# Two of every four message tiles gathered by TensorE, with one-hot comparisons four chunks wide

## The chip, the cores and the metric

The kernel runs on one core of one Trainium2 chip. The metric is the device time of one execution in microseconds (us). The kernel before was run three times: 3272.55, 3278.92 and 3280.07 us, median 3278.92. One further execution was profiled, and its trace is what the rows below are read from.

## The reference

A graph of 3,125 nodes with 64 features and 103,125 edges, sorted by destination, goes through four residual layers. The change lies in the last one, and in a piece of preparation placed inside the third. The last layer computes, with `h = relu(layernorm(x))`:

```python
edge_in = concatenate([edge_feat, hid[src]], axis=1)
msg = relu(edge_in @ W1 + b1)
msg_sum = segment_sum(msg, dst, num_segments=3125)
reduced = msg_sum / maximum(count, 1)
x = x + relu(concatenate([reduced, hid], axis=1) @ W2 + b2)
```

The term `hid[src] @ W1[64:] + b1` is worked out once per node by the stage before, as a table with one row per node (`message_table` in device memory, `gt` in SBUF). So an edge needs the row of its source node, plus its own feature product, then the relu and the sum by destination.

## The kernel before

Edges are taken in tiles of 256 (`TE`), two halves of 128. There are 403 tiles (`T1`). Sums by destination go over blocks of 64 nodes; each visit of a block by a tile is one step of sums, 451 in all (`V2`). `stage_messages` is one loop written out for every engine; at step i TensorE does, in this order:

- the product of edge features of tile t = i (L2088; L2082 on a "picked" tile),
- the pick matmuls that `chunks_of_step(i)` lists (L2095),
- the sums of visit v = i - 2, four instructions (L2104).

A tile gets its source rows in one of two ways. On an ordinary tile GpSimd gathers them from device memory with two indirect DMAs (L2056), up to 8 tiles ahead, and VectorE adds them to the product (L2186). On a picked tile TensorE makes them: `on_pe(t)` says which, the last two of every `GP` = 7 tiles from the second seven on. For the two picked tiles of a group (512 edges) VectorE compares the 512 source indices, less a shift, with the node numbers of each of 25 chunks of 128 nodes (L2192, one instruction a chunk, giving a 128 x 512 one-hot matrix in float16). TensorE multiplies each one-hot with that chunk of the table, split into two float16 halves (L2095), adding the 25 into one bank. ScalarE copies the sum to `hT` (L2122), and TensorE adds it onto the tile's product through `comb` (L2085).

SP loads the 512 indices, broadcast to all partitions, as int32 (L2046); ScalarE turns them into float16 keys with the partition's own number taken off (L2117). 32 one-hot buffers go round. Two banks hold products (`psM`), four hold sums (`psA`), two hold picked rows (`psH`). ScalarE also makes the one-hots of the destinations (L2137, L2143) and applies the relu (L2131, L2128); VectorE adds each visit's sums to the accumulator (L2198). `split()` on VectorE (L2161 to L2174) makes the two float16 halves of the table once, at its step 3; TensorE's first pick waits for it.

Three stages earlier, `stage_attend_tables` prepares the attention layer. Its engines work side by side and the stage ends when the last of them is done; GpSimd's three additions (L1407 to L1411) stand at its end.

Of the kernel before, what the change touches and what calls it, by code (L numbers as in the profile page):

```python
# [8 lines left out]
F16 = mybir.dt.float16  # L9
# [8 lines left out]
P = 128  # L18
NODES = 3125
EDGES = 103125  # L20
D = 64
# [1286 lines left out]
CENTER = NODES // 2  # L1308
AG = 16
# [45 lines left out]
def stage_attend_tables(nc, m, keep, s_in, x_out, q_out, w_in, w1, w2, w3, bp, bb2, b3, g2, b2, b1, x_t, q_t):  # L1355

    with ExitStack() as ctx:
# [11 lines left out]
        s_wt = sem("at_wt"); s_u = sem("at_u"); s_wo = sem("at_wo"); s_zero = sem("at_zero")  # L1369
        turned = sem("at_turned"); copied = sem("at_copied"); q_done = sem("at_q_done"); q_ready = sem("at_q")  # L1370
# [6 lines left out]
        def _(sp):  # L1377
# [10 lines left out]
            for g in range(NG):  # L1388
                sp.wait_ge(x_taken0, g + 1)
                sp.wait_ge(x_taken1, g + 1)  # L1390
                j = slice(2 * GROUP * g, 2 * GROUP * g + 2 * len(chunks(g)))
                sp.dma_start(q_t[j, :, :].rearrange("j p n -> p j n"), q_all[:, j, :]).then_inc(q_out, 16)
            sp.wait_ge(w_in, WEIGHTS_IN)
# [54 lines left out]
        def _(act):  # L1448
            act.wait_ge(s_zero, 2)
# [20 lines left out]
        def _(dve):  # L1470
# [8 lines left out]
            ins.then_inc(s_wo, 1)  # L1479
            dve.tensor_reduce(gm, hn.rearrange("p a d -> p (a d)"), op=ALU.max, axis=X, apply_absolute_value=True).then_inc(m.max_in, 1)  # L1480
            dve.wait_ge(s_zero, 2)
            for g in range(NG + 1):
                if g < NG:
# [3 lines left out]
                    dve.tensor_scalar(qf[g % 2][:, 0:n], m.PB[2 + g % 2][:, 0:n], bq_c, float(D) ** -0.5, ALU.add, ALU.mult).then_inc(q_ready, 1)  # L1487
                if g >= 1:
# [475 lines left out]
GP = 7  # L1964
HOT = 32
# [17 lines left out]
def chunks_of_step(i):  # L1983

    return [(q, a) for q, t in enumerate(chains()) for u in range(GP) if i == t - 5 + u for a in range(u * NCH // GP, (u + 1) * NCH // GP)]


def stage_messages(nc, m, keep, w1, w_out, b_out, o_in, ef_t, src, g_t):

    with ExitStack() as ctx:  # L1990
# [16 lines left out]
        hot = [take(TE).bitcast(F16) for _ in range(HOT)]  # L2007
        keyI = [take(2 * TE).bitcast(I32) for _ in range(2)]
        key = [take(TE).bitcast(F16) for _ in range(2)]
        hT = [take(TE).bitcast(F16) for _ in range(2)]  # L2010
        down, downI = take(1), m.colsN[:, 7, 0:1].bitcast(I32)
        gmax, gtop, one_row = take(1), take(1, 1), take(P, 1)
        wexp = take(1).bitcast(I32)
        psM = [halves(m.PB[0][:, 0:2 * D]), halves(m.PB[1][:, 0:2 * D])]
        psA = [m.PB[2 + i][0:BD, 0:MW] for i in range(4)]
# [9 lines left out]
        key_ready, hot_ready, hot_used, h_copied = m.key_ready, m.hot_ready, m.hot_used, m.h_copied  # L2025
# [5 lines left out]
        def _(sp):  # L2031
# [3 lines left out]
            for t in range(T1):  # L2035
# [6 lines left out]
                if t % GP == 0 and on_pe(t + 2 * GP - 2):  # L2042
                    q = chains().index(t + GP)
                    wait(sp, key_ready, Q0 + q - 1)
                    edges = src[(t + 2 * GP - 2) * TE:(t + 2 * GP) * TE]
                    sp.dma_start(keyI[q % 2], edges.partition_broadcast(P)).then_inc(m.landed_q[q % 2], 16)  # L2046
# [14 lines left out]
        def _(pe):  # L2061
# [7 lines left out]
            for i in range(V2 + 2):  # L2069
                t = i  # L2070
                if t < T1:
                    pe.wait_ge(m.landed_e[t % R], before(t) + landed(t))
                    if t >= 2:
                        if on_pe(t - 2):
                            pe.wait_ge(m_ready, t - 1)
                        else:
                            pe.wait_ge(added, pool_tiles(t - 1))
                    both = psM[t % 2].rearrange("p s c -> p (s c)")
                    if on_pe(t):
# [3 lines left out]
                        for s in range(2):  # L2083
                            e = (t % GP - (GP - 2)) * TE + s * P
                            ins = pe.matmul(psM[t % 2][:, s, :], hT[q % 2][:, e:e + P], comb, start=False, stop=True, skip_group_check=True)  # L2085
# [3 lines left out]
                for q, a in chunks_of_step(i):  # L2089
# [5 lines left out]
                    pe.matmul(psH[q % 2], table[:, a, :, :].rearrange("p s d -> p (s d)"), hot[n % HOT],  # L2095
                              start=(a == 0), stop=(a == NCH - 1)).then_inc(hot_used, 1)
                v = i - 2
                if v >= 0:
# [3 lines left out]
                    wait(pe, acc_ready, v - 3)  # L2102
                    for s in range(2):
                        ins = pe.matmul(psA[v % 4], oh[v % 4][:, s, :], M[:, bass.ds(slot, 1), s, :].rearrange("p t c -> p (t c)"),  # L2104
# [257 lines left out]
```

## Time and profile before

| | |
|---|---|
| median of three runs | 3278.92 us |
| profiled execution: its own time | 3277.56 us |
| profiled execution: span of the instructions | 3275.8 us |
| message tiles, first to last product (L2088) | 2422.85 to 3196.26 us |
| message stage's sums after the last tile, then output | 3201.79 to 3275.8 us |
| busy share of the span, TensorE / VectorE / ScalarE / GpSimd | 82 / 67 / 50 / 48 % |

The span leaves out 1.8 us of the execution's own time. Busy shares are means over all four layers; the change acts on about a quarter of the span, and what bounds that quarter must be read from its own stretch. "PE" is TensorE's matmuls, "PEld" its weight loads, "DVE" VectorE, "ACT" ScalarE, "POOL" GpSimd, "SP" the queue that issues most transfers.

### The profile page before, as it was taken

The numbers are of one execution on the slowest core, as the hardware profiler recorded it, in microseconds if no ns is written. First come the engines' busy times: TensorE is split into PE (matmuls) and PEld (weight loads), VectorE is DVE, ScalarE is ACT, GpSimd is POOL, SyncE is SP. The second block draws the span as 40 slices with busy tenths as digits, with TensorE's granted clock in tenths as the row PEclk, the third lists the DMA queues.
The fourth block names the chain that finished last, engine by engine and source line by source line (L and its number), as shares of the span: only waits on it lengthen the run. The fifth ranks groups of instructions, "written<-read, shape, count | busy, mean of one in ns | idle before, by whom it ended". The sixth has DMA issues, their size and how long they took to land. (4 is left out here: it accounts for less than half of the span.)

```text
span 3275.8 us, 70668 instructions
## 1 busy us (share of the span) xinstructions
PE 2693.3 (82%) x18331; PEld 1815.5 (55%) x18331; DVE 2187.2 (67%) x7716; ACT 1623.9 (50%) x4731; POOL 1571.5 (48%) x1644
## 2 busy tenths in 40 slices
PE   2777777799996799488889888899968888888888
PEld 1566665455553344267777777777844444444446
DVE  6999997566665224567777777777876565566552
ACT  1788886133332000145555555555655555555555
POOL 2111110144442000277777777776037777777770
PEclk6999999899998899689999999999879999999995
DMA  1222222255558766233333333333123333333320
GB/s 37 76 89 89 91 89 74 66 196 198 199 197 322 304 241 240 73 75 85 80 81 84 81 80 85 81 80 72 29 54 82 80 79 79 79 79 79 79 69 13
DMA packets 412218, 349.46 MB, mean 107 GB/s; under 512 B 174824, under 2 KB 342984, under 8 KB 411880
## 3 DMA queue, kind: packets, MB, share of 16 engines
q1 hardware_dynamic: 360296, 286.03, 27.6%
q0 software_dynamic: 42176, 44.91, 7.1%
q10 hardware_dynamic: 9408, 14.34, 1.2%
q8 instruction: 173, 2.83, 0.4%
q14 instruction: 165, 1.35, 0.1%
HBM read 259.07 MB, written 86.00 MB: 105 GB/s over the span
## 5 line engine op out<-in xcount | busy, mean ns | idle before, releaser
L1579 POOL DMA_INDIRECT big<-row_table,src x710 | 676.7, 953 | 217.3 <-issue 169.9
L2056 POOL DMA_INDIRECT big<-message_table,src x582 | 605.8, 1041 | 242.2 <-issue 174.1
L507 PE MATMUL banks<-work 128*128 128x226 f16 x1197 | 312.5, 261 | 104.8 <-ACT banks L538 43.7
L2095 PE MATMUL banks<-big 128*128 128x512 f16 x1400 | 372.4, 384 | 7.6 <-DVE big L2174 7.6
L2192 DVE TENSOR_SCALAR big<-big 128x512 f16<-128x512 f16 x1400 | 349.3, 307 | 28.9 <-ACT big L2117 28.3
L899 PE MATMUL banks<-big,work 128*128 128x512 f16 (+1 forms) x1750 | 344.4, 354 | 17.0 <-DVE work L1041 17.0
L964 POOL TENSOR_TENSOR work<-work 128x400 f16<-128x400 f32 x196 | 180.3, 946 | 272.4 <-DVE work L1033 205.8
L1724 DVE TENSOR_REDUCE big<-banks 128x1 f32<-128x256 f32 x451 | 190.3, 422 | 172.7 <-PE banks L1622 159.6
L1622 PE MATMUL banks<-big 97*128 x902 | 302.5, 418 | 0.0
L508 PE MATMUL banks<-work 128*128 128x200 f16 x1197 | 300.8, 251 | 0.0
L509 PE MATMUL banks<-work 128*128 128x200 f16 x1197 | 298.7, 250 | 0.0
L2186 DVE TENSOR_TENSOR big<-banks,big 128x128 f32<-128x128 f32 x291 | 84.0, 289 | 285.3 <-issue 174.8
L1665 ACT ACTIVATE big<-big 128x1 f32<-128x1 f32 x451 | 91.5, 203 | 351.6 <-DVE big L1735 339.4
L2137 ACT ACTIVATE big<-iotaH,rel 128x64 f32<-128x64 f16 x902 | 259.0, 335 | 5.2 <-DVE big L2151 3.6
L450 POOL COPY work<-work 128x100 f16<-128x100 f16 x120 | 70.2, 586 | 398.2 <-DVE work L473 379.1
L2104 PEld LDWEIGHTS banks<-big 128*64 128x64 f32 x1804 | 152.5, 147 | 192.2 <-issue 191.1
L899 PEld LDWEIGHTS banks<-big,work 128*128 128x128 f16 x1750 | 156.0, 100 | 184.4 <-DVE work L1041 17.3
L2131 ACT ACTIVATE big<-big 128x128 f32<-128x128 f32 x291 | 89.9, 309 | 332.5 <-DVE big L2186 315.0
L1115 PE MATMUL banks<-big,work 128*128 128x512 f16 x900 | 203.4, 387 | 56.2 <-DVE work L1199 52.1
L2104 PE MATMUL banks<-big 128*64 x1804 | 216.9, 247 | 22.8 <-issue 11.7
L1605 PE MATMUL banks<-ident,big 128*97 128x128 f32 x710 | 146.7, 290 | 100.1 <-issue 69.5
L928 ACT CAST work<-work 128x400 f16<-128x400 f32 x196 | 100.7, 525 | 240.2 <-DMA work<-weights_dense 239.5
(372 smaller groups left out, 6293.9 us busy)
## 6 DMA issues: line engine op xcount, KB each, us to landing
big<-weights_halves SPq DMA_DIRECT2D x10, 6400.0 KB, 24.0
weights_dense<-work SPq DMA_DIRECT2D x196, 200.0 KB, 1.9
work<-weights_dense SPq DMA_DIRECT2D x196, 200.0 KB, 2.6
weights_halves<-work SPq DMA_DIRECT2D x98, 400.0 KB, 2.7
big<-q_table SPq DMA_DIRECT2D x451, 64.0 KB
big<-in_ef SPq DMA_DIRECT2D x403, 64.0 KB
big<-in_src SPq DMA_DIRECT2D x56, 256.0 KB
big<-in_ea SPq DMA_DIRECT2D x403, 32.0 KB
```

Source lines behind the costliest of these rows:

```text
L507: pe.matmul(to(CW, CW + CAW), rows[:, 0, t, :], cols[:, t, :], start=False, stop=True, skip_group_check=True)
L508: pe.matmul(to(0, CW), rows[:, 1, t, :], cols[:, t, 0:CW], start=False, stop=True, skip_group_check=True)
L509: pe.matmul(to(0, CW), rows[:, 2, t, :], cols[:, t, 0:CW], start=False, stop=True, skip_group_check=True).then_inc(vis_done, 1)
L899: ins = pe.matmul(m.PB[c % 4][:, 0:width(c)], z[k][:, a, :, :], m.counts(c)[:, a, :], start=(a == 0), stop=(a == NCH - 1))
L1115: pe.matmul(out, z[l % 2][:, a, :, :], weights[:, :, s, a * BP:(a + 1) * BP], start=(a == 0 and s == 0), stop=False)
L1579: po.indirect_dma_start(rows[:, t % RT, s, 0:D], None, x_t.rearrange("a p c -> (a p) c"), bass.IndirectOffsetOnAxis(ap=m.src2[:, s, t:t + ...
L1622: pe.matmul(psS[v % 3], qT[v % R][0:XW, :], XF[0:XW, bass.ds(slot, 1), :].rearrange("p t e -> p (t e)"), start=False, stop=True).then_inc( ...
L2056: po.indirect_dma_start(G[n % R][:, s, :], None, g_t.rearrange("a p c -> (a p) c"), bass.IndirectOffsetOnAxis(ap=m.src2[:, s, t:t + 1], ax ...
L2095: pe.matmul(psH[q % 2], table[:, a, :, :].rearrange("p s d -> p (s d)"), hot[n % HOT], start=(a == 0), stop=(a == NCH - 1)).then_inc(hot_u ...
L2104: ins = pe.matmul(psA[v % 4], oh[v % 4][:, s, :], M[:, bass.ds(slot, 1), s, :].rearrange("p t c -> p (t c)"), start=(s == 0), stop=(s == 1))
L2137: ins = nc.scalar.activation(away[v % 2][:, s, :], m.iotaH[:, 0:BD], ACT.Abs, bias=m.rel2[:, s, v:v + 1], scale=-1.0)
L2192: dve.tensor_scalar(hot[n % HOT], key[q % 2], float(P * a - CENTER), None, ALU.is_equal).then_inc(hot_ready, 1)
```

## The change

- `GP` goes from 7 to 4: the last two of every four tiles are picked, and the 25 chunks of a group's chain are spread over four steps instead of seven (6, 6, 6 and 7 of them).
- The comparisons come in batches of four chunks: five shifted float16 copies of all source indices (`src - CENTER - 128 k`, k = 0 to 4) are made once, in `stage_attend_tables`, and written to device memory (`keys_t`). A group's keys are loaded as five rows of 512 per partition; one instruction compares four rows with one number per partition (`place`), which stands for chunks a to a + 3. Six instructions of 2048 columns and one of 512 replace 25 of 512.
- ScalarE's conversion L2117 is gone, with its semaphore; SP's key load waits for the comparisons of the group before last.
- One one-hot buffer per chunk (25) instead of 32 in rotation.
- Three banks for products and three for sums, instead of two and four; the waits on them follow.
- `split()` comes at VectorE's step 2 instead of 3.
- New in `stage_attend_tables`: a load of `src` from ScalarE's queue, five VectorE instructions of 806 columns, a 1 MB write to `keys_t` on SP's queue, and SP's wait until it has landed.

The diff, with signatures and the parts that only pass names through left out:

```diff
@@ -1306,6 +1306,7 @@
 CENTER = NODES // 2
+SHIFTS = 5
 AG = 16
@@ -1367,6 +1368,9 @@
         s_wt = sem("at_wt"); s_u = sem("at_u"); s_wo = sem("at_wo"); s_zero = sem("at_zero")
+        s_keys = sem("at_keys")
+        srcI = take(EPAD // P).bitcast(I32)
+        shifted = take(SHIFTS * EPAD // P // 2).bitcast(F16).rearrange("p (k f) -> p k f", k=SHIFTS)
         turned = sem("at_turned"); copied = sem("at_copied"); q_done = sem("at_q_done"); q_ready = sem("at_q")
@@ -1390,6 +1394,10 @@
                 sp.dma_start(q_t[j, :, :].rearrange("j p n -> p j n"), q_all[:, j, :]).then_inc(q_out, 16)
+                if g == NG - 3:
+                    sp.wait_ge(s_keys, SHIFTS)
+                    sp.dma_start(keys_t.rearrange("k (p f) -> p k f", p=P), shifted).then_inc(m.first_landed[1], 16)
+            sp.wait_ge(m.first_landed[1], 32)
             sp.wait_ge(w_in, WEIGHTS_IN)
@@ -1446,6 +1454,7 @@
         def _(act):
+            act.dma_start(srcI, src.rearrange("(p f) -> p f", p=P)).then_inc(m.first_landed[0], 16)
             act.wait_ge(s_zero, 2)
@@ -1477,6 +1486,8 @@
             ins.then_inc(s_wo, 1)
+            dve.wait_ge(m.first_landed[0], 32)
+            dve.tensor_scalar(shifted[:, 0, :], srcI, float(-CENTER), None, ALU.add).then_inc(s_keys, 1)
             dve.tensor_reduce(gm, hn.rearrange("p a d -> p (a d)"), op=ALU.max, axis=X, apply_absolute_value=True).then_inc(m.max_in, 1)
@@ -1485,6 +1496,10 @@
                     dve.tensor_scalar(qf[g % 2][:, 0:n], m.PB[2 + g % 2][:, 0:n], bq_c, float(D) ** -0.5, ALU.add, ALU.mult).then_inc(q_ready, 1)
+                if 1 <= g < SHIFTS:
+                    if g == 1:
+                        dve.wait_ge(s_keys, 1)
+                    dve.tensor_scalar(shifted[:, g, :], shifted[:, 0, :], float(-P * g), None, ALU.add).then_inc(s_keys, 1)
                 if g >= 1:
@@ -1961,8 +1976,10 @@
-GP = 7
-HOT = 32
+GP = 4
+BATCHES = ((0, 4), (4, 4), (8, 4), (12, 4), (16, 4), (20, 4), (24, 1))
+STEP_BATCHES = (BATCHES[0:2], BATCHES[2:4], BATCHES[4:5], BATCHES[5:7])
+KEY_ROW = 2 * TE + 2
@@ -1982,10 +1999,15 @@
-    return [(q, a) for q, t in enumerate(chains()) for u in range(GP) if i == t - 5 + u for a in range(u * NCH // GP, (u + 1) * NCH // GP)]
-
-
-def stage_messages(nc, m, keep, w1, w_out, b_out, o_in, ef_t, src, g_t):
+    return [(q, a) for q, t in enumerate(chains()) for u in range(GP) if i == t - GP + 1 + u for a in range(u * NCH // GP, (u + 1) * NCH // GP)]
+
+
+def batch_of_step(i):
+
+    return [(q,) + b for q, t in enumerate(chains()) if 0 <= i - t + GP - 1 < GP for b in STEP_BATCHES[i - t + GP - 1]]
+
+
+def stage_messages(nc, m, keep, w1, w_out, b_out, o_in, ef_t, keys_t, g_t):
@@ -2004,15 +2026,15 @@
         comb = take(D // 2).bitcast(F16)
-        hot = [take(TE).bitcast(F16) for _ in range(HOT)]
-        keyI = [take(2 * TE).bitcast(I32) for _ in range(2)]
-        key = [take(TE).bitcast(F16) for _ in range(2)]
+        hot = take(NCH * TE).bitcast(F16)
+        key = [take(SHIFTS * KEY_ROW // 2).bitcast(F16).rearrange("p (k e) -> p k e", k=SHIFTS)[:, :, 0:2 * TE] for _ in range(2)]
+        place = take(len(BATCHES))
         hT = [take(TE).bitcast(F16) for _ in range(2)]
-        down, downI = take(1), m.colsN[:, 7, 0:1].bitcast(I32)
+        downI = m.colsN[:, 7, 0:1].bitcast(I32)
         gmax, gtop, one_row = take(1), take(1, 1), take(P, 1)
         wexp = take(1).bitcast(I32)
-        psM = [halves(m.PB[0][:, 0:2 * D]), halves(m.PB[1][:, 0:2 * D])]
-        psA = [m.PB[2 + i][0:BD, 0:MW] for i in range(4)]
+        psM = [halves(m.PB[i][:, 0:2 * D]) for i in range(3)]
+        psA = [m.PB[3 + i][0:BD, 0:MW] for i in range(3)]
         psH = [m.PB[6], m.PB[7]]
@@ -2022,7 +2044,7 @@
         acc_ready = sem("ms_acc")
-        key_ready, hot_ready, hot_used, h_copied = m.key_ready, m.hot_ready, m.hot_used, m.h_copied
+        hot_ready, hot_used, h_copied = m.hot_ready, m.hot_used, m.h_copied
         Q0, N0 = len(PICKS), NCH * len(PICKS)
@@ -2041,9 +2063,12 @@
                     q = chains().index(t + GP)
-                    wait(sp, key_ready, Q0 + q - 1)
-                    edges = src[(t + 2 * GP - 2) * TE:(t + 2 * GP) * TE]
-                    sp.dma_start(keyI[q % 2], edges.partition_broadcast(P)).then_inc(m.landed_q[q % 2], 16)
+                    if q == 0:
+                        sp.wait_ge(m.first_landed[1], 32)
+                    if q >= 2:
+                        sp.wait_ge(hot_ready, N0 + NCH * (q - 1))
+                    edges = keys_t[:, (t + 2 * GP - 2) * TE:(t + 2 * GP) * TE]
+                    sp.dma_start(key[q % 2], edges.partition_broadcast(P)).then_inc(m.landed_q[q % 2], 16)
@@ -2070,19 +2095,19 @@
                     pe.wait_ge(m.landed_e[t % R], before(t) + landed(t))
-                    if t >= 2:
-                        if on_pe(t - 2):
-                            pe.wait_ge(m_ready, t - 1)
+                    if t >= 3:
+                        if on_pe(t - 3):
+                            pe.wait_ge(m_ready, t - 2)
                         else:
-                            pe.wait_ge(added, pool_tiles(t - 1))
-                    both = psM[t % 2].rearrange("p s c -> p (s c)")
+                            pe.wait_ge(added, pool_tiles(t - 2))
+                    both = psM[t % 3].rearrange("p s c -> p (s c)")
                     if on_pe(t):
...
                             e = (t % GP - (GP - 2)) * TE + s * P
-                            ins = pe.matmul(psM[t % 2][:, s, :], hT[q % 2][:, e:e + P], comb, start=False, stop=True, skip_group_check=True)
+                            ins = pe.matmul(psM[t % 3][:, s, :], hT[q % 2][:, e:e + P], comb, start=False, stop=True, skip_group_check=True)
                         ins.then_inc(m_done, 1)
@@ -2092,16 +2117,16 @@
                     pe.wait_ge(hot_ready, N0 + n + 1)
-                    pe.matmul(psH[q % 2], table[:, a, :, :].rearrange("p s d -> p (s d)"), hot[n % HOT],
+                    pe.matmul(psH[q % 2], table[:, a, :, :].rearrange("p s d -> p (s d)"), hot[:, 2 * TE * a:2 * TE * (a + 1)],
                               start=(a == 0), stop=(a == NCH - 1)).then_inc(hot_used, 1)
...
                     pe.wait_ge(oh_ready, v + 1)
-                    wait(pe, acc_ready, v - 3)
+                    wait(pe, acc_ready, v - 2)
                     for s in range(2):
-                        ins = pe.matmul(psA[v % 4], oh[v % 4][:, s, :], M[:, bass.ds(slot, 1), s, :].rearrange("p t c -> p (t c)"),
+                        ins = pe.matmul(psA[v % 3], oh[v % 4][:, s, :], M[:, bass.ds(slot, 1), s, :].rearrange("p t c -> p (t c)"),
                                         start=(s == 0), stop=(s == 1))
@@ -2110,11 +2135,6 @@
                 t = i
-                if t % GP == 0 and on_pe(t + 2 * GP - 2):
-                    q = chains().index(t + GP)
-                    act.wait_ge(m.landed_q[q % 2], -(-(V2 - q % 2) // R) * 16 + 16 * (q // 2 + 1))
-                    wait(act, hot_ready, N0 + NCH * (q - 1))
-                    nc.scalar.activation(key[q % 2], keyI[q % 2], ACT.Identity, bias=down).then_inc(key_ready, 1)
                 if on_pe(t + 2) and t % GP == GP - 4:
@@ -2125,7 +2145,7 @@
                         act.wait_ge(s_max, 5)
-                        ins = nc.scalar.activation(M[:, t % RT, :, 0:D], psM[t % 2], ACT.Relu, scale=m.unscale)
+                        ins = nc.scalar.activation(M[:, t % RT, :, 0:D], psM[t % 3], ACT.Relu, scale=m.unscale)
                     else:
@@ -2145,7 +2165,8 @@
             chain = m.dve_step.on(dve)
-            dve.tensor_copy(down, downI)
+            for b, (a, _) in enumerate(BATCHES):
+                dve.tensor_scalar(place[:, b:b + 1], downI, -1.0, float(P * a - 2 * CENTER), ALU.mult, ALU.add)
             dve.memset(w_e, 0.0)
@@ -2174,7 +2195,7 @@
             for i in range(-1, V2 + 3):
-                if i == 3:
+                if i == 2:
                     split()
@@ -2183,19 +2204,20 @@
                         dve.wait_ge(m_ready, [u for u in range(t) if not on_pe(u)][-4] + 1)
-                    dve.tensor_tensor(T[n % 4], psM[t % 2], G[n % R], ALU.add).then_inc(added, 1)
-                for q, a in chunks_of_step(i + 2):
-                    n = q * NCH + a
+                    dve.tensor_tensor(T[n % 4], psM[t % 3], G[n % R], ALU.add).then_inc(added, 1)
+                for q, a, n in batch_of_step(i + 2):
                     if a == 0:
-                        dve.wait_ge(key_ready, Q0 + q + 1)
-                    wait(dve, hot_used, N0 + n - HOT + 1 if n >= HOT else 0)
-                    dve.tensor_scalar(hot[n % HOT], key[q % 2], float(P * a - CENTER), None, ALU.is_equal).then_inc(hot_ready, 1)
+                        dve.wait_ge(m.landed_q[q % 2], -(-(V2 - q % 2) // R) * 16 + 16 * (q // 2 + 1))
+                    if q:
+                        dve.wait_ge(hot_used, N0 + NCH * (q - 1) + a + n)
+                    dve.tensor_scalar(hot[:, 2 * TE * a:2 * TE * (a + n)], key[q % 2][:, 0:n, :], place[:, BATCHES.index((a, n)):BATCHES.index((a, n)) + 1],
+                                      None, ALU.is_equal).then_inc(hot_ready, n)
                 v = i - 3
...
                     a = acc[:, bass.ds(own.of(v), 1), :].rearrange("p j c -> p (j c)")
-                    dve.tensor_tensor(a, a, psA[v % 4], ALU.add).then_inc(acc_ready, 1)
+                    dve.tensor_tensor(a, a, psA[v % 3], ALU.add).then_inc(acc_ready, 1)
```

## Rows read from the trace of the kernel before

**Rows 1.** Windows: busy us (instructions) of each engine, granted clock, DMA share, GB/s

```profile
2439.55:3196.30 756.75, 646.57 (x3999) 359.30 (x3997) 449.83 (x2063) 439.03 (x1696) 585.06 (x564) 0.99 0.32 78
800.00:1000.00 200.00, 192.09 (x1117) 103.88 (x1116) 135.79 (x275) 65.07 (x130) 91.65 (x100) 1.00 0.61 201
```

**Rows 2.** Groups by line, 2400 to 3276 us: busy, mean ns, idle before

```profile
L2056 POOL DMA_INDIRECT big<-message_table,src x582 | 605.8, 1041 | 242.2 <-issue 174.1 <-POOLq L1756 65.0 <-DVE big L2186 3.0
L2095 PE MATMUL banks<-big 128*128 128x512 f16 x1400 | 372.4, 384 | 7.6 <-DVE big L2174 7.6
L2192 DVE TENSOR_SCALAR big<-big 128x512 f16<-128x512 f16 x1400 | 349.3, 307 | 28.9 <-ACT big L2117 28.3 <-PE banks L2095 0.3
...
L2095 PEld LDWEIGHTS banks<-big 128*128 128x128 f16 x1400 | 131.8, 99 | 102.5 <-DVE big L2192 29.4 <-DVE big L2174 7.9 <-issue 1.9
L2198 DVE TENSOR_TENSOR big<-big,banks 64x65 f32 x451 | 93.1, 206 | 32.8 <-PE banks L2104 28.0 <-DVE big L2198 3.0 <-issue 1.0
...
L2186 DVE TENSOR_TENSOR big<-banks,big 128x128 f32<-128x128 f32 x291 | 84.0, 289 | 285.3 <-issue 174.8 <-PE banks L2088 78.0 <-DMA big<-message_table,src 29.8
```

**Rows 3.** GpSimd in order of time: start, length, instruction, idle before

```profile
2799.78 1.81 POOL L2056 DMA_INDIRECT big<-message_table,src  x1 [0.30 <-issue]
2801.89 0.95 POOL L2056 DMA_INDIRECT big<-message_table,src  x1 [0.30 <-issue]
...
2813.22 1.80 POOL L2056 DMA_INDIRECT big<-message_table,src  x1 [0.30 <-issue]
```

**Rows 4.** TensorE in order of time, a stretch in which it never waits

```profile
2450.50 0.49 PE L2082 MATMUL banks<-big 128*128 128x128 f32 x2
...
2452.22 0.49 PE L2082 MATMUL banks<-big 128*128 128x128 f32 x2
...
2453.72 0.49 PE L2088 MATMUL banks<-big 128*128 128x128 f32 x2
...
2457.03 0.49 PE L2088 MATMUL banks<-big 128*128 128x128 f32 x2
...
2458.47 0.49 PE L2088 MATMUL banks<-big 128*128 128x128 f32 x2
...
2461.57 0.49 PE L2082 MATMUL banks<-big 128*128 128x128 f32 x2
```

**Rows 5.** VectorE in order of time: two runs of four comparisons

```profile
2813.08 0.88 DVE L2192 TENSOR_SCALAR big<-big 128x512 f16<-128x512 f16 x4
...
2814.02 0.88 DVE L2192 TENSOR_SCALAR big<-big 128x512 f16<-128x512 f16 x4
```

**Rows 6.** Groups by line, whole trace: one-source VectorE instructions of other shapes

```profile
L1697 DVE TENSOR_SCALAR big<-big,rel 128x128 bf16<-128x128 f16 x678 | 175.0, 269 | 12.7 <-issue 12.1
...
L2173 DVE CAST big<-big 128x1600 f16<-128x1600 f32 x1 | 1.8, 1819 | 0.0
...
L2171 DVE TENSOR_SCALAR big<-big,scales 128x1600 f32<-128x1600 f32 x1 | 1.0, 1048 | 0.0
...
L801 DVE TENSOR_SCALAR work<-work 128x1600 f32<-128x1600 f32 x1 | 1.0, 994 | 0.0
```

**Rows 7.** TensorE in order of time: the stage's start and its end

```profile
2432.51 1.46 PE L2095 MATMUL banks<-big 128*128 128x512 f16 x3 [7.62 <-DVE big L2174]
...
2439.55 0.49 PE L2088 MATMUL banks<-big 128*128 128x128 f32 x2
...
3196.26 0.80 PE L2088 MATMUL banks<-big 128*128 128x128 f32 x2
...
3201.79 4.78 PE L2104 MATMUL banks<-big 128*64 x24 [1.71 <-ACT big L2131]
```

**Rows 8.** GpSimd, then VectorE, in order of time, `stage_attend_tables`

```profile
1358.05 0.13 POOL L1401 IOTA colsN<- 128x1 int32 x1 [7.46 <-issue]
...
1378.91 3.55 POOL L1411 TENSOR_TENSOR work<-work 128x1600 f32<-128x1600 f32 x1
...
1368.10 0.89 DVE L1493 COPY big<-banks 97x512 f32<-97x512 f32 x2
```

More of the change, by code:

```diff
@@ L1352, in gathers_before, with stage_attend_tables @@
     return -(-(len(FETCHED) - n % R) // R) * 16
-def stage_attend_tables(nc, m, keep, s_in, x_out, q_out, w_in, w1, w2, w3, bp, bb2, b3, g2, b2, b1, x_t, q_t):
+def stage_attend_tables(nc, m, keep, s_in, x_out, q_out, w_in, w1, w2, w3, bp, bb2, b3, g2, b2, b1, x_t, q_t, src, keys_t):
     with ExitStack() as ctx:
@@ L2301, in build @@
         g_t = scratch("message_table", [NCH, P, D])
+        keys_t = nc.dram_tensor("shifted_keys", [SHIFTS, EPAD], F16, kind="Internal").ap()
         xv = x.rearrange("(a p) d -> p a d", p=P)
@@ L2317, in build @@
         stage_attend_tables(nc, m, keep, at_in, x_out, q_out, w_in, L2_gnn_W1, L2_gnn_W2, L3_gnn_W1[D:, :], L2_gnn_bp, L2_gnn_b2, L3_gnn_b1,
-                            L2_gnn_ln2_g, L2_gnn_ln2_b, L2_gnn_b1, x_t, q_t)
+                            L2_gnn_ln2_g, L2_gnn_ln2_b, L2_gnn_b1, x_t, q_t, src, keys_t)
         stage_attend(nc, m, keep, x_out, q_out, ea, ea_t, src, x_t, q_t)
         stage_nodes(nc, m, keep, g_t)
-        stage_messages(nc, m, keep, L3_gnn_W1[0:D, :], L3_gnn_W2, L3_gnn_b2, o_in, ef, src, g_t)
+        stage_messages(nc, m, keep, L3_gnn_W1[0:D, :], L3_gnn_W2, L3_gnn_b2, o_in, ef, keys_t, g_t)
         stage_output(nc, m, keep, o_in, out)
```

## The prediction

> **What bounds the kernel now.** I read three kinds of view of the message stage. First the windows: over tiles 5 to 402 (756.75 us) TensorE is busy 646.57 us, GpSimd 585.06, VectorE 449.83 and ScalarE 439.03, at a granted clock of 0.99 [rows 1]. No engine is full there, so the shares do not name the bound. Then the groups by line: GpSimd's gathers waited for VectorE only 3.0 us in all, while their idle time is nearly all "issue" [rows 2]. That is an engine that goes from one instruction to the next. Then GpSimd's timeline: a gather takes 0.95 us plus 0.30 before it, and once in each group of seven tiles one takes 1.80 [rows 3]. Two such long ones are 13.44 us apart: ten gathers by 1.25 us, plus 0.86. For seven tiles that is 1.92 us a tile, and the stage's mean is 756.75 / 397 = 1.906 us a tile [rows 1]. So **GpSimd's gathers set the pace**.
>
> Last TensorE's timeline, in the early stretch in which gathers are still ahead and TensorE never waits [rows 4]. The reader should see that it has a pace of its own, only a little faster: seven tiles from 2450.50 to 2461.57, 11.07 us, 1.58 a tile. Two plain tiles with four picks each take 3.31 us (2453.72 to 2457.03), 1.655 each, one with three 1.44; so a pick costs 0.215 us, and everything else on a plain tile 1.655 - 4 x 0.215 = 0.795. Picked tiles take 1.72 with four picks and 1.50 with three: 0.857 without their picks.
>
> **The change, part by part.**
>
> *Gathers.* 198 tiles are picked instead of 112 (two of each of 99 groups), so 205 are gathered: 410 gathers for 582. A group of four needs 4 x 1.25 = 5.0 us of GpSimd instead of 7.7. Its stall stops mattering if nothing slower takes over.
>
> *Picks.* A group's chain is 25 matmuls for 512 edges however many tiles lie between. There are now 99 chains instead of 56: 2475 matmuls instead of 1400. A group of four costs TensorE 2 x 0.795 + 2 x 0.857 + 25 x 0.215 = **8.68 us, 2.17 a tile**, against the 1.906 at which the stage runs now [rows 1, 4]. This is the central term: TensorE, not GpSimd, becomes the bound, and it is slower than the old one.
>
> For the pick's price the Trainium skill has another figure. Its page "TensorE: Matmul & The Clock Gate", section "Back-to-back issue gap", gives about 131 ns for each matmul of 512 columns in a sustained stream. By it, as an estimate, a group would cost 6.58 us; the rows give 0.215 us, and I go by them.
>
> *Comparisons.* VectorE's price for a one-source instruction: 1600 columns take 1819 ns at one column at a time and 994 at two, so about 155 ns fixed and 1.04 ns a column at the slow rate [rows 6]. The 512-column comparison, 0.88 us for four, spaced 0.20 [rows 5], is at four columns at a time. A scalar read per partition adds 1048 - 994 = 54 ns and keeps the rate (L2171 against L801); L1697, float16 with such a scalar, has a mean of 269 for 128 columns against 307 for L2192's 512, what is left after those 54 ns being 384 columns at a quarter rate [rows 2, 6]. A batch of 2048 then takes 155 + 533 + 54 = 0.74 us, spaced about 0.66. Six and the short one: 4.2 us a group. With two additions (0.29) and four accumulations (0.21) [rows 2] VectorE has 5.6 of 8.68 us: hidden. The input as four rows with a gap no row shows; lower bound 0.66, upper bound one column at a time, 2.26. I take the lower, the nearest rows being the same operation and types.
>
> *Waits.* Comparisons for step i + 2 come in VectorE's step i, behind step i's addition and ahead of the accumulation of visit i - 3. The heaviest step has 0.29 + 1.32 + 0.21 = 1.8 us against TensorE's 2.1, so it stays ahead. The new wait `hot_used` is for picks of the chain before, issued at least a step earlier; behind it stand the accumulations, for which TensorE (three banks of sums) waits two steps later. ScalarE's copy of the chain's sum now waits at the start of the step in which the chain ends; behind it are that step's relu and one-hots (about 1.4 us), needed two steps of 2.17 later. The third bank of products relaxes a wait; the lost bank of sums tightens one that is met by then. All this at nothing; if one fell behind, it would cost tenths of a microsecond in each of 99 groups.
>
> *Keys.* ScalarE loses 56 conversions and gains 43 copies; it is far from full. A group loads 655 KB of keys instead of 262, as 1 KB rows, now every 8.68 us. With 4 x 65.5 KB of features and 4 x 32.8 of gathered rows this is about 121 GB/s, against 78 now, and 201 elsewhere in the same program [rows 1]. SP asks for them some four steps ahead (over 8 us), with features queued behind, which have seven tiles in hand: hidden.
>
> *Preparation.* In `stage_attend_tables` VectorE gets about 2 us more and SP a 1 MB write. GpSimd ends that stage at 1382.46, its chain beginning with an index at 1358.05 and the last addition starting at 1378.91; VectorE ends its copies at 1368.99 [rows 8]. The 13.5 us between cover both. 0 us, bound +3, if VectorE's wait for the load of `src` holds up GpSimd's maximum.
>
> *Start.* Before, TensorE's first pick is at 2432.51, after `split()`, and step 5 begins at 2439.55 [rows 7]. `split()` is one step earlier, but behind five batches and a larger key load; I leave its end where it is. TensorE then stands in step 1: 12 picks at half the clock (0.43), a product and a sum group, 6.4 us, so step 3 begins at 2438.9.
>
> *Steps 3 to 402.* 2463 picks x 0.215 = 529.5; 198 picked tiles x 0.857 = 169.7; 199 plain x 0.795 = 158.2; two steps without picks 1.6: together 859.0. Tile 402's product is at 3297.9 instead of 3196.26 [rows 7]: **+101.6**.
>
> *Tail.* Now the last sums start 5.5 us after that product, because the last gather lands late [rows 7]; with gathers long landed about 2.2 us: **-3.3**.
>
> Sum: 3277.56 + 101.6 - 3.3 = 3375.9 for the profiled execution's own time. The median before lies 1.4 us above that execution, so 3377.
>
> **The rivals.**
>
> *A. TensorE bound, as above:* 3377, own range 3360 to 3395 (0.005 us on a pick is 12 us, 0.03 on a step 12). 0.80.
>
> *B. VectorE becomes the bound.* If the gapped rows cost the comparison its rate: at two columns at a time a batch is 1.2 us, 8.1 to 9.0 a group, 3377 to 3410; at one, 15.1 to 15.6 a group, 99 groups, about 4040. For it: no row has this input. Against: L1697 and L2171. 0.05.
>
> *C. GpSimd stays the bound because long comparisons hold it off.* The 1.80 us gather stands beside eight comparisons nearly in a row [rows 3, 5]. If a gather could never be written while VectorE compares, a group would take 5.0 + 4.2 = 9.2 us: 2.30 a tile, 3430. Now some 55 us of the gathers' 605.8 are beyond 0.95 each, against 1400 x 0.21 = 294 of comparing [rows 2]: a fifth, which gives 5.8 a group. 0.04. The Trainium skill has this as a rule ("SBUF — State Buffer", section "SBUF: two separate sides"): VectorE in a two-port mode and GpSimd take one port pair by turns, the loser "fully blocks". The long gathers agree; the rule alone speaks for C.
>
> *D. Something in the four-step order is late* (the copy of the chain, keys, the sums' banks): 0.5 us a group gives 3425. 0.05.
>
> *E. Faster: the pick's price falls when six or seven stand in a row.* Place: L2095. It decides from (4 x 1.906 - 3.30) / 25 = 0.173 us a pick downwards. The floor is its weight load, 0.099 [rows 2]; halfway between, at 0.136, a group takes 6.7 us, 1.68 a tile, 92 us less than now in 397 tiles: about 3190. Against it: a fourth pick costs the same 0.215 as the others [rows 4]. 0.04. The skill's figure above, if it held here, would be this case.
>
> *F. No difference:* gain and loss cancel, at 0.173 to 0.18 a pick or the like. 0.02.
>
> **Numbers.** 3377 is A's. The range 3352 to 3408 holds A with its bounds and half of B; outside are E, F, C, D and a column at a time, 0.17. About 0.3% is what a measurement of this kernel can tell from no change. Faster 0.04 (E), same 0.02 (F), slower 0.94.
>
> **What would show it.** In the profile after: TensorE's tiles 2.17 us apart four-step groups of 8.68, hardly any idle time; picks spaced 0.215; GpSimd idle some 3 us a group, waiting for VectorE's additions; a batch of comparisons 0.74 us long; the stage before attention no longer. Wrong would be: TensorE waiting for comparisons (B), gathers back to back (C), picks closer than 0.173 (E), or a granted clock well under 0.99 in the stage.

## The result, and the profile after

The changed kernel takes **3380.52 us** in the median of four runs (3378.6 to 3382.63), the kernel before 3279.49 beside it (3272.55 to 3288.03): a ratio of 1.0307, 95% interval 1.0282 to 1.0332, 3.1% slower. The profiled execution took 3380.56 us, its span is 3378.8. The prediction was 3377. All medians below are of executions at the usual granted clock: one execution of `wide_gp7`, 3364.7 us at a mean clock of 0.811 where its others have 0.932 to 0.938, is left out.

The changed kernel in its steady stretch, from eleven microseconds after its first pick to the end of its picks (in the form of [rows 1], whose first stretch is the kernel before: busy us of TensorE, its weight loads, VectorE, ScalarE and GpSimd, then clock, DMA share and GB/s):

```profile
2447.96:3297.49 849.53, 849.53 (x5184) 456.16 (x5183) 526.72 (x1267) 431.39 (x1659) 496.59 (x390) 1.00 0.45 121
```

TensorE is busy for all 849.53 of 849.53 us. Before, no engine was full, and GpSimd's back-to-back gathers were the pace. The granted clock is 1.00, the DMA traffic 121 GB/s.

The groups by line of the changed kernel, 2400 us to its end, as in [rows 2] (busy us, mean ns, then the idle time before and who ended it):

```profile
L2120 PE MATMUL banks<-big 128*128 128x512 f16 x2475 | 600.2, 380 | 8.0 <-DVE big L2195 8.0
L2081 POOL DMA_INDIRECT big<-message_table,src x410 | 518.4, 1264 | 408.5 <-DVE big L2207 247.4 <-issue 96.0 <-POOLq L1771 65.0
L2213 DVE TENSOR_SCALAR big<-big 128x2048 f16<-128x2048 f16 x594 | 425.1, 742 | 0.7 <-PE banks L2120 0.4 <-issue 0.2
...
L2213 DVE TENSOR_SCALAR big<-big 128x512 f16<-128x512 f16 x99 | 33.6, 339 | 0.0
```

There are 2475 picks, and none waited after the first (the 8.0 us is the stage's start). The 410 gathers wait 247.4 us for VectorE's additions. A comparison four chunks wide takes 742 ns. The waits of the changed kernel, 2400 to 3300 us (total, times, longest), say who waits for whom:

```profile
DVE big L2207 <- PE banks L2113: 248.4, 199, 3.2
ACT big L2142 <- PE banks L2120: 248.4, 99, 2.6
POOL big L2081 <- DVE big L2207: 247.4, 94, 2.7
```

It is a chain that ends at TensorE: GpSimd waits for the addition that frees a buffer, and that addition and ScalarE's copy of the chain's sum wait for TensorE. TensorE itself waits in this view only before the stage and at its start (the same 8.0 us), not once the picks run. TensorE in order of time, one group of four in the changed kernel (compare [rows 4]):

```profile
2802.54 0.49 PE L2113 MATMUL banks<-big 128*128 128x128 f32 x2
2802.86 1.46 PE L2120 MATMUL banks<-big 128*128 128x512 f16 x6
2804.25 0.45 PE L2129 MATMUL banks<-big 128*64 x4
2804.62 0.49 PE L2107 MATMUL banks<-big 128*128 128x128 f32 x2
...
2806.77 0.49 PE L2107 MATMUL banks<-big 128*128 128x128 f32 x2
...
2808.92 0.49 PE L2113 MATMUL banks<-big 128*128 128x128 f32 x2
2809.24 1.67 PE L2120 MATMUL banks<-big 128*128 128x512 f16 x7
...
2811.22 0.49 PE L2113 MATMUL banks<-big 128*128 128x128 f32 x2
```

From 2802.54 to 2811.22, four products later, is **8.68 us**, in steps of 2.08, 2.15, 2.15 and 2.30. Six picks in a row take 1.46 us, seven 1.67: one more costs 0.21, as the fourth one did before. GpSimd in the same stretch of the changed kernel:

```profile
2801.32 1.21 POOL L2081 DMA_INDIRECT big<-message_table,src  x1 [2.67 <-DVE big L2207]
2802.83 1.30 POOL L2081 DMA_INDIRECT big<-message_table,src  x1 [0.31 <-issue]
2804.44 1.54 POOL L2081 DMA_INDIRECT big<-message_table,src  x1 [0.30 <-issue]
2806.28 1.06 POOL L2081 DMA_INDIRECT big<-message_table,src  x1 [0.30 <-issue]
2810.01 1.21 POOL L2081 DMA_INDIRECT big<-message_table,src  x1 [2.67 <-DVE big L2207]
```

Four gathers are 5.11 us of busy time, 1.3 more than 4 x 0.95; every one of them is stretched a little. Yet the engine then has 2.4 us with nothing to do but wait (2.67 less the usual 0.30). VectorE beside it, changed kernel:

```profile
2800.76 0.29 DVE L2207 TENSOR_TENSOR big<-banks,big 128x128 f32<-128x128 f32 x1 [2.24 <-PE banks L2113]
2800.96 1.41 DVE L2213 TENSOR_SCALAR big<-big 128x2048 f16<-128x2048 f16 x2
```

Two batches take 1.41 us and one 0.742, so they are spaced 0.67. The stage's start and end in the changed kernel, for [rows 7]:

```profile
2437.19 2.74 PE L2120 MATMUL banks<-big 128*128 128x512 f16 x6 [8.00 <-DVE big L2195]
...
3302.39 0.49 PE L2113 MATMUL banks<-big 128*128 128x128 f32 x2
```

First pick to last product: 865.20 us, against 3196.26 - 2432.51 = 763.75 before, **+101.45**. Last product to the end of the span: 76.41 against 79.54, **-3.1**. That leaves +4.7 before the stage (2437.19 against 2432.51).

### The profile page after: what moved, and what is told of

Its sections match the earlier page's. It is cut to its first block and busy times, and to the rows that moved or that the text cites. A ratio compares the mean times of both kernels' runs of the same rounds, so it can differ in the third digit from the quotient of the medians.

```text
span 3378.8 us, 72723 instructions
## 1 busy us (share of the span) xinstructions
PE 2908.3 (86%) x19578; PEld 1920.1 (57%) x19578; DVE 2273.6 (67%) x6934; ACT 1621.7 (48%) x4718; POOL 1498.2 (44%) x1472
## 5 line engine op out<-in xcount | busy, mean ns | idle before, releaser
L2081 POOL DMA_INDIRECT big<-message_table,src x410 | 518.4, 1264 | 408.5 <-DVE big L2207 247.4
L2120 PE MATMUL banks<-big 128*128 128x512 f16 x2475 | 600.2, 380 | 8.0 <-DVE big L2195 8.0
L2213 DVE TENSOR_SCALAR big<-big 128x2048 f16<-128x2048 f16 (+1 forms) x693 | 451.1, 685 | 0.7 <-PE banks L2120 0.4
L2120 PEld LDWEIGHTS banks<-big 128*128 128x128 f16 x2475 | 229.3, 98 | 210.0 <-DVE big L2195 8.3
L450 POOL COPY work<-work 128x100 f16<-128x100 f16 x120 | 84.4, 707 | 383.1 <-DVE work L473 364.0
L2207 DVE TENSOR_TENSOR big<-banks,big 128x128 f32<-128x128 f32 x205 | 59.8, 292 | 252.3 <-PE banks L2113 249.8
```

Source lines behind the costliest of these rows:

```text
L2081: po.indirect_dma_start(G[n % R][:, s, :], None, g_t.rearrange("a p c -> (a p) c"), bass.IndirectOffsetOnAxis(ap=m.src2[:, s, t:t + 1], ax ...
L2213: dve.tensor_scalar(hot[:, 2 * TE * a:2 * TE * (a + n)], key[q % 2][:, 0:n, :], place[:, BATCHES.index((a, n)):BATCHES.index((a, n)) + 1], ...
```

## The experiments

Two theories were left to separate. **T**: TensorE's own time for a group is the bound at four, GpSimd's gathers (each lengthened by VectorE's comparisons) at six and seven. **G**: the comparisons, four chunks wide, lengthen the gathers so much that these cost the time at four as well. The window from 2500 to 3100 us shows a stage at its steady pace; means and waits below are of that stretch unless the text says otherwise. A gather nobody holds off is taken as 0.947 us, and what a mean lies above it is called lost.

**1 to 3. The wide comparisons with other groups** (`wide_gp7`, `wide_gp6`, `wide_gp5`). The changed kernel, but two tiles picked of seven (below), six or five:

```diff
-GP = 4
+GP = 7
-STEP_BATCHES = (BATCHES[0:2], BATCHES[2:4], BATCHES[4:5], BATCHES[5:7])
+STEP_BATCHES = [[b for b in BATCHES if u * NCH // GP <= b[0] < (u + 1) * NCH // GP] for u in range(GP)]
```

> The changed kernel with GP = 7 again; everything else of the change stays (wide comparisons, shifted keys, three banks each). Each batch of comparisons stands at the step in which its first chunk is picked. Theory T (the slower of two paces sets the tiles: TensorE's 0.795 or 0.857 us a tile plus 25 picks of 0.215 a group; GpSimd's 1.25 us a gather plus what wide comparisons take from it): TensorE would need 11.06 us a group of seven, GpSimd 12.5 plus 1.3 to 2.5 of time locked out (1.3 is what the changed kernel shows a group), so GpSimd sets 13.8 to 15.0 us a group: 3300 to 3375 us, 3320 likeliest. Rival W (the change's slowdown lies in the wide comparisons, keys and banks, not in the picks): about 3380, as the changed kernel. Rival N (width costs the gathers nothing more than before): 3279, as the kernel before.

Measured: 3288.34 us, ratio 1.0021 (1.0011 to 1.0031).

> The changed kernel with GP = 6. Theory T: TensorE 4 x 0.795 + 2 x 0.857 + 25 x 0.215 = 10.27 us a group of six, 1.71 a tile; GpSimd eight gathers, 10.0 plus 1.3 to 2.5 locked out, 1.88 to 2.08 a tile, so GpSimd sets the pace: 3270 to 3345, 3290 likeliest. Rival W: 3380. Rival N: 10.9 a group, 1.81 a tile, 3240.

Measured: 3304.2 us, 1.0078 (1.0061 to 1.0095).

> The changed kernel with GP = 5. Theory T: TensorE 3 x 0.795 + 2 x 0.857 + 25 x 0.215 = 9.47 us a group of five, 1.895 a tile; GpSimd six gathers, 7.5 plus 1.3 to 2.5, 1.76 to 2.0 a tile: the two meet; 3275 if TensorE sets the pace, up to 3310 if the lockout is at its upper end. Rival W: 3380.

Measured: 3268.86 us, 0.9962 (0.9948 to 0.9976).

At seven the whole rewriting of keys and comparisons costs 0.2%, so the 3.1% lie in four instead of seven. The gathers' mean is 1059 ns against 1044 before, where I had expected much more: the time lies below the expected range of 3300 to 3375. GpSimd is the pace at seven and at six. The groups by line of the kernel with six, 2500 to 3100 us:

```profile
L2081 POOL DMA_INDIRECT big<-message_table,src x403 | 477.9, 1186 | 122.9 <-issue 114.6 <-DVE big L2207 8.2
L2120 PE MATMUL banks<-big 128*128 128x512 f16 x1257 | 331.7, 389 | 57.1 <-DVE big L2213 56.9
```

The gathers waited 8.2 us for anything; 8 x (1.186 + 0.305) = 11.93 us a group, 1.99 a tile, worse than the 1.906 of before: a tile has 1.33 gathers instead of 1.43, but each loses more. TensorE also waits 56.9 us for comparisons, and 70.3 with seven. I read that as a consequence, since GpSimd never stops and so sets the pace: VectorE's additions wait for a gathered tile, and the comparisons stand behind them. No run tests that reading alone. At five, TensorE is busy 600.00 of 600 us. By the prediction's terms five tiles are 3 x 0.795 + 2 x 0.857 + 25 x 0.215 = 9.47 us, 1.895 a tile, 0.011 less than before, 4 us in 397 tiles, and 3 more from the tail. Measured is 12 us less in the medians and 7.6 between the profiled spans (3268.2 for 3275.8). The time lies 6 us below the lowest that was expected, 3275; that part of the gain stays unexplained.

**4. The old comparisons at six** (`narrow_gp6`): the kernel before, two of six.

```diff
-GP = 7
+GP = 6
-    return [(q, a) for q, t in enumerate(chains()) for u in range(GP) if i == t - 5 + u for a in range(u * NCH // GP, (u + 1) * NCH // GP)]
+    return [(q, a) for q, t in enumerate(chains()) for u in range(GP) if i == t - GP + 2 + u for a in range(u * NCH // GP, (u + 1) * NCH // GP)]
```

> The kernel before with GP = 6 alone (narrow comparisons, its own banks and keys; the chain ends one step after the group's start as before). Theory T: GpSimd 8 x 1.25 + 0.86 = 10.9 us a group of six, 1.81 a tile against 1.906 now; TensorE 1.71: 38 us less than before, about 3241 (3235 to 3260). Rival: if any larger share of picks costs time (TensorE the bound already), 3279 or more.

Measured: 3261.09 us, 0.994 (0.9923 to 0.9957). Of the right sign, but half of the expected gain. Its gathers from 2500 to 3100 us:

```profile
L2056 POOL DMA_INDIRECT big<-message_table,src x428 | 471.2, 1101 | 130.5 <-issue 127.7 <-DVE big L2186 2.7
```

The mean is 1101 ns, 8 x 0.154 = 1.23 us lost a group, where I had taken the 0.86 of the kernel before.

**5. Fewer picks at four** (`gp4_20picks`): the changed kernel without five of each chain's 25 matmuls; all else stays.

```diff
+KEPT = [a for a in range(NCH) if a not in (5, 11, 17, 23, 24)]
...
+                    if a not in KEPT:
+                        continue
```

> The changed kernel without five of the 25 pick matmuls of each chain (chunks 5, 11, 17, 23 and 24); all comparisons are still made, so rows of those chunks are missing from the messages. Theory T (TensorE sets the pace, 0.215 us a pick): 99 x 5 x 0.215 = 106 us less, about 3274. Rival V or G (VectorE or GpSimd or a late hand-over sets it): no change, about 3380.

Measured: 3270.59 us, 0.9977 (0.9966 to 0.9988). Against 1.0307 that is 0.033 of 3277.25, 108 us for 99 x 5 = 495 picks: 0.218 us each. The whole price of a pick shows in the time, so T holds, and within these 108 us nothing else takes over as the bound.

**6, 7. Half of the gathers at four and at seven** (`gp4_half_gathers` from the changed kernel, `gp7_half_gathers` from the one before). The second half's rows are zeros, so the sums are not the right ones.

```diff
-                for s in range(2):
+                for s in range(1):
...
-                    dve.wait_ge(m.landed_g[n % R], 2 * gathers_before(n) + landed(n, 2))
+                    dve.wait_ge(m.landed_g[n % R], 2 * gathers_before(n) + landed(n, 1))
```

> The changed kernel with only the first of the two gathers of each gathered tile; the second half's rows are zeros written once. Theory T: GpSimd is not on the path, no change: 3380 (3374 to 3386). Rival G (wide comparisons hold gathers off, GpSimd sets the pace): 205 gathers fewer by 1.5 us, up to 100 us less.

Measured: 3379.85 us, 1.0309 (1.0292 to 1.0326).

> The kernel before with only the first of the two gathers of each gathered tile; the second half's rows are zeros written once. Theory T: GpSimd set the pace before; without it TensorE does, at 11.06 us for seven tiles, 1.58 a tile for 1.906: 397 x 0.326 = 129 us less, about 3148. Rival: if TensorE or VectorE already set the pace before, 3279.

Measured: 3145.93 us, 0.9598 (0.9582 to 0.9614).

The same edit is worth nothing at four and 4% at seven. That is T's picture: GpSimd is off the path after and on it before. It also measures TensorE's own pace at seven: with the gathers out of the way a group of seven takes 11.08 us in mid-stage, from picked tile to picked tile:

```profile
2800.84 0.49 PE L2082 MATMUL banks<-big 128*128 128x128 f32 x2
...
2811.92 0.49 PE L2082 MATMUL banks<-big 128*128 128x128 f32 x2
```

[Rows 4] had 11.07 in the early stretch. By it the gain is 397 x (1.906 - 1.581) = 129 us and 3 of tail; 0.0402 of 3277.25 is 132.

**8. The comparisons cut up at four** (`gp4_narrow`): each batch of 2048 columns as four instructions of 512.

```diff
-                    dve.tensor_scalar(hot[:, 2 * TE * a:2 * TE * (a + n)], key[q % 2][:, 0:n, :], ...).then_inc(hot_ready, n)
+                    for c in range(n):
+                        dve.tensor_scalar(hot[:, 2 * TE * (a + c):2 * TE * (a + c + 1)], key[q % 2][:, c, :], ...).then_inc(hot_ready, 1)
```

> The changed kernel with each batch of four comparisons cut into four of one chunk (25 of 128 x 512 a chain, still with one number per partition). VectorE then needs 25 x 0.26 + 1.4 = 7.9 us of a group's 8.68. Theory T: TensorE still sets the pace, 3380 (up to 3400 if VectorE falls late in the step with eight chunks, 2.6 us against TensorE's 2.1). Rival V (comparisons are what sets the pace at GP = 4): clearly slower than 3400.

Measured: 3378.3 us, 1.0306 (1.0289 to 1.0323). VectorE and GpSimd both get much worse and the time does not move. GpSimd of this kernel in order of time:

```profile
2802.47 0.94 POOL L2081 DMA_INDIRECT big<-message_table,src  x1 [0.30 <-issue]
2803.72 1.70 POOL L2081 DMA_INDIRECT big<-message_table,src  x1 [0.30 <-DVE big L2207]
2805.72 2.68 POOL L2081 DMA_INDIRECT big<-message_table,src  x1 [0.31 <-issue]
2809.79 1.07 POOL L2081 DMA_INDIRECT big<-message_table,src  x1 [1.39 <-DVE big L2207]
```

The gather of 2.68 us stands beside eight comparisons in a row. All gathers together lose some 267 us (410 at a mean of 1.598) against 130 in the changed kernel (1.264), and still each group ends in a wait of GpSimd for VectorE. This settles the case against G: twice the loss, and no time.

**9 to 12. Taking the loss away.** If comparisons that follow each other without a gap hold a gather, then a wait between them should free it. On a picked tile VectorE has no addition to wait for, so its comparisons of one step run into those of the next. The edit lets it wait there, ahead of the step's comparisons, for the tile's product on TensorE, in the kernel before with seven (`gp7_paced`), with six (`gp6_paced`), and with groups of six and five in turn, without it (`mix65`) and with it (`mix65_paced`). Only the wait is shown; the code of the mixed groups is left out:

```diff
+                if 0 <= t < T1 and on_pe(t):
+                    dve.wait_ge(m_done, t + 1)
```

> The kernel before with one wait more: on a picked tile VectorE, which has no addition there, waits for that tile's product before its comparisons, so that they no longer run through three steps without a gap. Theory L (a gather is held off while VectorE compares without a gap; 0.86 us a group of seven): the long gather shrinks to about half its excess or less, 0.06 us a tile, 3255 (3250 to 3270). Rival: what holds the gather off is the sum of comparison time, not its being in one piece: no change, 3279.

Measured: 3274.32 us, 0.9985 (0.9976 to 0.9993), about a fifth of the gain that was expected.

> The kernel before with GP = 6 and the same wait. Its unpaced form took 3261 with 1.26 us a group of six beyond 0.95 us a gather, most of it in one gather of 2.0 to 2.2 us. Theory L: about half of that comes back, 0.1 us a tile, 3222 (3215 to 3240), where TensorE's own 1.71 us a tile is near. Rival: no change, 3261, or slower if VectorE's comparisons come late for TensorE.

Measured: **3195.56 us, 0.9739** (0.9725 to 0.9753), far better than expected and the best kernel of the study.

> The kernel before with groups of six and five tiles in turn, two picked in each, narrow comparisons. Theory T: eleven tiles cost TensorE 10.27 + 9.47 = 19.74 us (1.795 a tile) and GpSimd 14 x 1.25 + 2 x 1.26 = 20.0 (1.82): the two paces nearly meet, about 20 us less than groups of six alone, 3240 (3235 to 3262). If the two engines' waits add instead of covering each other: 3262 or more.

Measured: 3244.17 us, 0.9885 (0.9869 to 0.9902).

> The same with the wait that paces the comparisons. Theory T and L: GpSimd falls to about 1.75 a tile, TensorE's 1.795 sets the pace: 3235 (3228 to 3245), 45 us less than the kernel before.

Measured: 3229.7 us, 0.9844 (0.983 to 0.9858).

One wait gives 5 us at seven and 66 at six (0.994 - 0.9739 = 0.0201 of 3280). The groups by line, 2500 to 3100 us, first of the paced kernel with six:

```profile
L2056 POOL DMA_INDIRECT big<-message_table,src x468 | 458.6, 980 | 142.6 <-issue 142.6
L2095 PE MATMUL banks<-big 128*128 128x512 f16 x1460 | 372.5, 379 | 0.0
L2194 DVE TENSOR_SCALAR big<-big 128x512 f16<-128x512 f16 x1462 | 350.5, 304 | 59.3 <-PE banks L2085 59.3
```

then of the paced kernel with seven:

```profile
L2056 POOL DMA_INDIRECT big<-message_table,src x447 | 465.3, 1041 | 136.2 <-issue 133.2 <-DVE big L2186 3.0
...
L2194 DVE TENSOR_SCALAR big<-big 128x512 f16<-128x512 f16 x1117 | 279.0, 308 | 24.3 <-ACT big L2117 21.9 <-PE banks L2085 1.9
```

The number to see is what the new wait did. It is for L2085, the last matmuls of a picked tile's product. With six it held VectorE 59.3 us in 600, and the gathers' mean fell from 1101 to 980 ns. With seven it held it 1.9 us: VectorE reached it late nearly every time, little was spread, and the mean stayed at 1041 (1044 before). VectorE of the paced kernel with six, in order of time, one picked tile and two plain ones:

```profile
2800.98 1.10 DVE L2194 TENSOR_SCALAR big<-big 128x512 f16<-128x512 f16 x5 [0.65 <-PE banks L2085]
2802.00 0.21 DVE L2200 TENSOR_TENSOR big<-big,banks 64x65 f32 x1
2802.64 0.29 DVE L2186 TENSOR_TENSOR big<-banks,big 128x128 f32<-128x128 f32 x1 [0.43 <-PE banks L2088]
2802.85 1.01 DVE L2194 TENSOR_SCALAR big<-big 128x512 f16<-128x512 f16 x4
2803.78 0.20 DVE L2200 TENSOR_TENSOR big<-big,banks 64x65 f32 x1
2804.30 0.29 DVE L2186 TENSOR_TENSOR big<-banks,big 128x128 f32<-128x128 f32 x1 [0.32 <-PE banks L2088]
```

Each step has its gap, 0.32 to 0.65 us. What a gap does can be read from where the gathers begin. In the kernel before, 445 gathers begin between 2500 and 3100 us. 270 of them begin while no comparison is under way, and none of these takes longer than 0.957 us, although in 210 of them comparisons start before they end. The 175 that begin during a comparison take 1.195 us in the mean. One of the first kind, in the kernel before, GpSimd and then VectorE:

```profile
2804.47 0.94 POOL L2056 DMA_INDIRECT big<-message_table,src  x1 [0.30 <-issue]
...
2804.67 1.06 DVE L2192 TENSOR_SCALAR big<-big 128x512 f16<-128x512 f16 x4
```

With groups of six and without the wait, 192 of 427 gathers begin during a comparison, at a mean of 1.291 us and up to 2.21. With the wait it is 240 of 467, at 1.014 and at most 1.07. So the wait does not keep gathers from beginning during comparisons; it shortens the runs that they begin in. (The wide comparisons also lengthen gathers that begin up to half a microsecond before one, to 1.33 us at most.)

A group of six then costs GpSimd 8 x (0.980 + 0.305) = 10.28 us, and TensorE 4 x 0.795 + 2 x 0.857 + 25 x 0.215 = 10.27: the two engines are level, 1.71 us a tile for 1.906, and TensorE is busy 600.00 of 600 us. With groups of six and five TensorE needs (10.27 + 9.47) / 11 = 1.795 a tile; there pacing takes the gathers' mean from 1152 to 961 ns, but only down to TensorE's pace, which is why this mixture loses to six throughout.

## Why the prediction was right, step by step

- **What bounds the kernel now**: GpSimd's gathers. Right; half of them gone gives 0.9598, with TensorE at 11.08 us a group.
- **The pick's price, 0.215 us.** Right, and it was the term that decided. In rows of six and seven it is 0.21 (1.46 to 1.67), taken out it gives 0.218. Rival E needed under 0.173. The Trainium skill's figure of about 131 ns ("TensorE: Matmul & The Clock Gate", section "Back-to-back issue gap") does not hold in this stream of weight loads and matmuls; here the trace decides against the page.
- **Steps 3 to 402, 859.0 us, and tile 402's product +101.6.** The group is 8.68 us as worked out. Step 3 begins at 2441.86 in the changed kernel, so these steps took 860.5, 1.5 more. The two steps before them took 4.7 us from the first pick where 6.4 was put: six picks stood at half the clock (2.74 us, granted 0.50 until 2439.70), not twelve. The two misses cancel, and from the first pick to the last product it is +101.45.
- **Comparisons, 0.74 us each, hidden.** 0.742 measured. The rows with a gap keep the rate that the prediction took (spaced 0.67 us for 2048 columns, as worked out), so rival B's premise was false here. The mean of 339 ns for the 512-column one against 307 before is also seen; it costs nothing here.
- **Gathers, 5.8 us a group.** Too small: 5.11 + 4 x 0.30 = 6.3. The loss to the comparisons is 1.3 us a group, not 0.8. It lies in GpSimd's 2.4 us of slack. Rival C put its mechanism rightly (the gathers do stretch) and its consequence wrongly: it needed 8.7 us and had 6.3; doubling the loss moved nothing. The Trainium skill's rule ("SBUF — State Buffer", section "SBUF: two separate sides"), that a VectorE instruction in a two-port mode and a GpSimd instruction exclude each other from a shared port pair, the later one blocked, agrees in part: gathers that begin during a comparison are stretched, but comparisons run beside gathers that began before them (210 of 270 in the kernel before, none over 0.957 us). And a rule on who is held off is not yet a bound.
- **Waits and keys, nothing.** Right; rival D would have shown as idle time of TensorE, and there is none. 121 GB/s as worked out.
- **Preparation 0, bound +3.** The stage itself grew by 0.5 us (38.06 to 38.58), within the bound. VectorE did wait for the load of `src`; in the changed kernel in order of time:

```profile
1354.53 0.81 DVE L1490 TENSOR_SCALAR big<-big 128x806 f16<-128x806 int32 x1 [3.14 <-DMA big<-in_src]
```

- **Start, step 3 at 2438.9.** It came at 2441.86, since the first pick was at 2437.19 and not at 2432.51. 4.3 of these 4.7 us were already there when `stage_attend_tables` began (1349.00 for 1344.69), ahead of all that the change touches; I take it for a difference of two executions: the two medians are 101.0 apart, against 98.3 predicted, and the profiled ones 103.0.
- **Tail, -3.3.** Measured -3.1. After the last product the sums go on with no wait over 0.53 us in the next 16, where the kernel before stood 1.71 twice. But the granted clock differs there too (0.85 from 3300 to 3310 us, 0.50 from 3196 to 3206 before), and the rows do not separate the two.

In sum: +101.45 - 3.1 + 4.7 is the +103.0 of the span (3275.8 to 3378.8), and 3377 stands against 3380.5. The mechanism and the term that decided were right; that the shorter start and the longer steps cancelled to 0.2 us was luck.

Of the expectations written later, five missed. `wide_gp5` came 6 us below its lowest figure, as said above. The other four missed for one reason. I took what a gather loses to VectorE as a constant: first as at least the 1.3 us of the changed kernel (`wide_gp7`), then as 0.86 us a group whatever the group (`narrow_gp6`), then as something that the new wait would remove by itself (`gp7_paced`), or only in part (`gp6_paced`). It is none of these. It depends on how long VectorE compares without a gap once a gather has begun in it. Which engine is behind seems to decide that. Why pacing is worth so much at six can be argued: once the gathers keep up with TensorE, VectorE is on time, meets its waits and leaves gaps, which keeps the gathers fast. At seven ten gathers need 10 x 1.25 = 12.5 us even when nobody holds them, more than TensorE's 11.07, so VectorE is always late and never paced. The rows show both ends of it (59.3 us of waiting, and 1.9), not the feedback itself. Why the wide comparisons lose more at six (1186 ns) than at seven (1059) stays open: at six 138 of 403 gathers begin during one, at a mean of 1.575 us, at seven 118 of 440, at 1.242, and no run added the wait to wide comparisons. Comparisons of another kind, or on another engine, were not tried.

## What to carry to other kernels

When work moves from an engine that is the bound to one that is nearly full, price it on the receiving engine, from a stretch in which that engine doesn't wait: here eleven microseconds of TensorE's timeline gave the added time, 98.3 us for 101.0. Size the share so that both engines come out level (at six, 10.28 and 10.27 us), rather than as far as it goes. And before dividing the work anew, see what slows the bound's single instruction: going from seven tiles to six gave 20 us, and one wait more, which put gaps into a neighbour's work, gave 66. The same wait at seven gave 5, because there the neighbour was late already and hardly ever met it.

## What the runs showed of the hardware

- A gather of 128 rows issued by GpSimd takes 0.94 to 0.95 us when nothing lengthens it, with 0.30 to the next. Beside VectorE's comparisons without a gap it takes up to 2.69 (`gp4_narrow`) and 3.03 (`mix65`). Means from 2500 to 3100 us ran from 0.961 (`mix65_paced`) to 1.639 us (`gp4_narrow`).
- In the kernel before, with comparisons of 512 columns, a gather's beginning decided: the 270 that began outside a comparison took at most 0.957 us whatever followed, the 175 that began in one 1.195 in the mean.
- Width alone does not set the loss. At four, instructions of 512 columns lost twice as much (267 us) as those of 2048 (130), with VectorE busy longer (703.3 us for 458.7). At six, in two kernels that differ in more than that, the wide ones lost more (1186 ns for 1101).
- A wait that holds VectorE for 10% of the time (59.3 of 600 us) went with gathers 11% shorter (1101 to 980 ns) and a kernel 66 us faster.
